# Expert regions cleared one batch sooner, experts chosen on logits, the last gate half first, one matrix addition a step

## What is computed

```python
x = x + ffn0(attention(x))       # layer 0
x = x + ffn1(lora_linear(x))     # layer 1

# attention: 8 query heads, 4 key/value heads of 64, a window of 256 in a paged cache
# ffn0: logits = clip(x @ gate_w.T, -50, 50); the top 2 of 8, softmax over those 2
#       expert e's matrix = W + 4096 weighted cells, scattered at mask_idx
# ffn1: probs = softmax(x @ gate_w); the top 2 of 8, scores divided by their sum, times alpha
#       expert e: fc2(gelu(fc1(x)))
```

## Time and profile before

| | us |
|---|---|
| median of 3 timed runs | 1142.62 (1139.97 to 1144.23) |
| the profiled execution, its own time | 1142.49 |
| its span, first to last instruction | 1140.7 |
| PE busy | 999.9 (88%) |
| DVE busy | 535.7 (47%) |
| ACT busy | 405.5 (36%) |
| POOL busy | 306.6 (27%) |

### The profile page before, as it was taken

How to read it: one execution, slowest core, us unless ns; L and a number is a source line. 1 busy time by engine, 2 the same in 40 slices (tenths; PEclk the granted TensorE clock), 3 DMA queues, 4 the chain that set the end, 5 groups by cost and what they waited for, 6 DMA issues and landing times.

```text
span 1140.7 us, 18892 instructions
## 1 busy us (share of the span) xinstructions
PE 999.9 (88%) x5042; PEld 678.0 (59%) x5043; DVE 535.7 (47%) x2106; ACT 405.5 (36%) x1185; POOL 306.6 (27%) x250
## 2 busy tenths in 40 slices
PE   5999949899999899808889997999289999999994
PEld 2464447677777677604444445666167777777772
DVE  5768874455455677442334442555423333333331
ACT  3434313555565555301111111112124444444440
POOL 3000140357654141111334440233202221122221
PEclk9989956899999999958999998999689999999998
DMA  8756540354453343238787745884443333333330
GB/s 266 238 215 214 198 162 21 94 131 112 127 157 114 112 153 112 75 130 228 210 221 125 137 84 166 303 332 160 149 139 67 68 62 72 72 65 67 57 59 2
DMA packets 82417, 156.25 MB, mean 137 GB/s; under 512 B 16023, under 2 KB 28999, under 8 KB 80768
## 3 DMA queue, kind: packets, MB, share of 16 engines
q1 hardware_dynamic: 40336, 86.99, 23.2%
q0 software_dynamic: 25520, 45.11, 19.1%
q10 hardware_dynamic: 16512, 23.60, 6.5%
HBM read 94.05 MB, written 73.19 MB: 147 GB/s over the span
## 4 chain that ended last, share of the span: by engine, by line
PE 64%; DVE 14%; issue 8%; DMA 7%; DVEq 2%; ACT 2%; SPq 2%; POOL 0%; ACTq 0%; POOLq 0%
PE ps L630 44%; PE ps L711 7%; PE ps L636 4%; DMA acc<-R,tok_i 4%; PE ps L701 3%; PE ps L694 3%; DVE R L1334 1%; DVE R L1326 1%; DVE R L1344 1%; PE ps L875 1%; DMA R<-rows 1%; DVE R L1337 1%; ACT R L977 1%; SPq L392 1%; SPq L391 1%
## 5 line engine op out<-in xcount | busy, mean ns | idle before, releaser
L630 PE MATMUL ps<-R 128*128 128x128 f32 (+4 forms) x2640 | 676.4, 413 | 20.1 <-DMA R<-in_x_t 11.5
L630 PEld LDWEIGHTS ps<-R 128*128 128x128 f32 x2640 | 395.9, 194 | 259.3 <-issue 242.4
L636 PE MATMUL ps<-ident,R 128*128 128x128 f32 x504 | 77.8, 286 | 67.2 <-DMA R<-rows 54.4
L602 POOL DMA_INDIRECT out_x<-R,tok_i x39 | 60.9, 1562 | 252.2 <-DVEq L1773 165.1
L530 POOL DMA_INDIRECT rows<-R,slot_i x64 | 67.1, 1048 | 203.5 <-DVEq L1521 180.6
L636 PEld LDWEIGHTS ps<-ident,R 128*128 128x128 f32 x504 | 62.2, 152 | 94.9 <-issue 77.1
L711 PEld LDWEIGHTS ps<-R 128*128 128x128 f32 x768 | 96.4, 199 | 20.0 <-ACT R L993 16.6
L711 PE MATMUL ps<-R 128*128 128x64 f32 x768 | 99.4, 281 | 4.8 <-ACT R L993 4.8
L1410 DVE CUSTOM_DVE_ANT_0 R<-ps,R 128x384 f32<-128x384 f32 x128 | 66.0, 553 | 75.2 <-issue 75.0
L987 ACT ACTIVATE R<-R,nmx 128x384 f32<-128x384 f32 x128 | 77.5, 607 | 58.8 <-DVE nmx L1410 58.7
L602 POOL DMA_INDIRECT acc<-R,tok_i x39 | 60.6, 1553 | 128.4 <-DVE R L1675 123.3
(11 more groups left out here) (281 smaller groups left out, 924.8 us busy)
## 6 DMA issues: line engine op xcount, KB each, us to landing
R<-rows SPq DMA_DIRECT2D x78, 258.0 KB, 3.4
R<-in_fc ACTq DMA_DIRECT2D x16, 1024.0 KB, 5.6
m_buf<-R SPq DMA_DIRECT2D x8, 1024.0 KB, 5.1
R<-m_buf SPq DMA_DIRECT2D x16, 512.0 KB, 3.9
R<-acc SPq DMA_DIRECT2D x32, 256.0 KB, 5.4
rows<-zrow SPq DMA_DIRECT2D x16, 258.0 KB, 3.7
new_kv<-R SPq DMA_DIRECT2D x16, 256.0 KB, 2.1
qn<-R SPq DMA_DIRECT2D x16, 256.0 KB, 2.5
```

The source lines that it names most:

```text
L602: po.indirect_dma_start(out=sums[s], out_offset=bass.IndirectOffsetOnAxis(ap=tok_i[:, s:s + 1], axis=0), in_=y_sb[s], in_offset=None, boun ...
L630: m = pe.matmul(out, lhs(k), rhs(k), start=(k == 0 and first), stop=(k == KC - 1 and last))
L636: m = pe.transpose(out[:, k * P:(k + 1) * P], src[:, k * P:(k + 1) * P], ident[:])
```

## The change

Six edits. (1) `ends`, split off from `tiles`, writes `end_i` and counts up `r_end` after the placing of the seventh batch. The zeros that SP writes there are 384 rows to an expert in place of 128 (up to 256 rows of the last batch may come before the 128), SP no longer waits for them, and POOL waits for them before it sends the last batch. (2) `choose` compares and multiplies in one operation per tile, which makes ten steps of it. Layer 1 chooses on the logits; the only exponential left is of the difference of the top two, `soft(i - 1)`, inside ACT's next pair. (3) At the end of attention PE projects the last tile's high half first, into bank 2, and the low half into bank 3. ACT in place of DVE copies the two halves out. (4) POOL issues 9 `cells` a round in rounds 1 and 2 and 10 in round 3. (5) DVE makes one addition in each step from period 4 step 2 on and the last two after `tiles`; SP fetches two pieces ahead of its `bk` wait and two behind it, from b = 4 on, and the first two at b = 3. (6) The loop over periods 1 to 4 is written out.

```diff
-            with eng.Fori(0, 2) as i:
-                period(2 * i + 1, "mid", 1, i)
-                period(2 * i + 2, "mid", 0, i)
...
+            for B in range(NB):
+                period(B, "first" if B == 0 else "last" if B == NB - 1 else "mid", B % 2, (B - 1) // 2)
...
             for b in range(NB - 1):
+                for m in range(4 * b - 14, 4 * b - 12) if b >= 4 else ():
+                    sp.wait_ge(S["m_done"], m - 1)
+                    fetch_m(m)
                 sp.wait_ge(S["bk"], uses(b, "mid" if b else "first")["q0"] + 1)
...
-                if b == 4:
+                if b == 3:
                     sp.wait_ge(S["mscat"], 16 * ST)
                     for m in range(2):
                         fetch_m(m)
-                if b >= 5:
-                    for m in range(7 * (b - 5) + 2, min(7 * (b - 4) + 2, 16)):
-                        sp.wait_ge(S["m_done"], m - 1)
-                        fetch_m(m)
+                for m in range(4 * b - 12, 4 * b - 10) if b >= 4 else ():
+                    sp.wait_ge(S["m_done"], m - 1)
+                    fetch_m(m)
...
                 for e in range(NE):
-                    end = sp.value_load(end_i[0:1, e:e + 1], min_val=0, max_val=ROWS - P * NE)
-                    sp.dma_start(rows_d[bass.ds(end, P), :].rearrange("p (h n) -> p h n", h=2),
-                                 zrow[:].unsqueeze(1).broadcast_to([P, 2, DX // 2])).then_inc(S["zrows"], 16)
-                sp.wait_ge(S["zrows"], 16 * NE * n)
+                    end = sp.value_load(end_i[0:1, e:e + 1], min_val=0, max_val=NE * REGION - 3 * P)
+                    sp.dma_start(rows_d[bass.ds(end, 3 * P), :].rearrange("(p a) (h n) -> p (a h) n", a=3, h=2),
+                                 zrow[:].unsqueeze(1).broadcast_to([P, 6, DX // 2])).then_inc(S["zrows"], 16)
...
-                t = 4 + 7 * (b - 1)
-                add = b <= 4
+                t = 4 + 9 * (b - 1)
+                add = b <= 3
...
-                    cells(t + 6)
+                    for u in range(t + 6, t + 9 if b < 3 else ST):
+                        cells(u)
             for b in (NB - 2, NB - 1):
                 po.wait_ge(S["r_slot"], b + 1)
+                if b == NB - 1:
+                    po.wait_ge(S["zrows"], 16 * NE)
                 for t in (2 * b, 2 * b + 1):
+                    if t == NT - 1:
+                        po.wait_ge(S["e_row"], 2)
...
-            project(at, "a1")
-            project(at, "h1")
+            pe.wait_ge(bc, at["o1"] + 1)
+            half("h1", 2).then_inc(S["e_in"], 1)
+            half("a1", 3).then_inc(S["e_in"], 1)
...
+                    if s == 0 and (not isinstance(i, int) or i > 0):
+                        soft(i - 1)
...
-                    TT(t1[:], src[:], b3(best2[:, c, :]), ALU.is_equal)
-                    ve.drain()
-                    TT(t1[:], t1[:], rb(rev[:]), ALU.mult)
+                    if c == 1:
+                        gap = TT(diff[:], best2[:, 1, :], best2[:, 0, :], ALU.subtract)
+                        if layer == 1:
+                            gap.then_inc(S["r_l"], 1)
+                    for t in range(2):
+                        ve.scalar_tensor_tensor(t1[:, t, :], src[:, t, :], best2[:, c, t:t + 1], rev[:], ALU.is_equal, ALU.mult)
...
+            def ends():
+                ve.drain()
+                CP(end_i[:], run[:])
+                ve.drain().then_inc(S["r_end"], 1)
...
-            ADDS = (2, 1, 2, 1, 1, 1, 1, 1)
...
                     if j == 7 and last:
+                        ends()
                         row_low(at, "a2", 2 * B)
-                    if isinstance(B, int) and 8 * B + j >= 42:
-                        for _ in range(ADDS[j]):
-                            next(adds, None)
+                    if 8 * B + j >= 34:
+                        next(adds)
...
                         for _ in place1(i - 1):
                             pass
+                        if not more:
+                            ends()
```

More of the change, by code:

```diff
@@ L281, in program @@
                 "last": ("a0", "h0", "o1", "a1", "h1", "o0", "rt", "a2"),
-                "after": ("h2", "o1", "a1", "h1", "rt")}
+                "after": ("h2", "o1", "rt")}
         NF, NM, NL = (len(USES[k]) for k in ("first", "mid", "last"))
@@ L290, in periods @@
         def periods(eng, period):
-            period(0, "first", 0, 0)
-            with eng.Fori(0, 2) as i:
-                period(2 * i + 1, "mid", 1, i)
-                period(2 * i + 2, "mid", 0, i)
-            period(5, "mid", 1, 2)
-            period(6, "mid", 0, 2)
-            period(NB - 1, "last", 1, 0)
+            for B in range(NB):
+                period(B, "first" if B == 0 else "last" if B == NB - 1 else "mid", B % 2, (B - 1) // 2)
         block = ctx.enter_context(nc.Block())
@@ L381, in _ @@
                         fetch_m(m)
-                if b >= 5:
-                    for m in range(7 * (b - 5) + 2, min(7 * (b - 4) + 2, 16)):
-                        sp.wait_ge(S["m_done"], m - 1)
-                        fetch_m(m)
+                for m in range(4 * b - 12, 4 * b - 10) if b >= 4 else ():
+                    sp.wait_ge(S["m_done"], m - 1)
+                    fetch_m(m)
+            for m in range(14, 16):
+                sp.wait_ge(S["m_done"], m - 1)
+                fetch_m(m)
             def zero_ends(n):
@@ L615, in _ @@
                 po.wait_ge(S["r_slot"], NB + b + 1)
+                if b == NB - 1:
+                    po.wait_ge(S["zrows"], 16 * NE * 2)
                 for t in (2 * b, 2 * b + 1):
@@ L719, in tail, with half @@
                 turn4(ps[:, 0, :], o_sb).then_inc(bk, 1)
+            def half(x, b):
+                lo, hi = (0, D // 2) if x[0] == "a" else (D // 2, DG)
+                return chunks(ps[:, b, 0:hi - lo], lambda k: o_t[:, k, :], lambda k: w_o[:, k, lo:hi])
             def project(at, x):
                 wait(pe, bc, at[x])
-                if x[0] == "a":
-                    chunks(ps[:, 0, 0:D // 2], lambda k: o_t[:, k, :], lambda k: w_o[:, k, 0:D // 2]).then_inc(bk, 1)
-                else:
-                    chunks(ps[:, 0, 0:DG - D // 2], lambda k: o_t[:, k, :], lambda k: w_o[:, k, D // 2:DG]).then_inc(bk, 1)
+                half(x, 0).then_inc(bk, 1)
             def cell_sums(at):
@@ L1039, in _ @@
             o_out(uses(NB, "after"), "1")
+            ac.wait_ge(S["e_lg"], 1)
+            ac.activation(a_rows[:, NT - 1, D // 2:D], ps[:, 2, 0:D // 2], ACT.Copy).then_inc(S["e_row"], 1)
+            ac.wait_ge(S["e_in"], 2)
+            ac.activation(a_rows[:, NT - 1, 0:D // 2], ps[:, 3, 0:D // 2], ACT.Copy).then_inc(S["e_row"], 1)
             ac.wait_ge(S["xs_sc"], 32 * NT)
@@ L1083, in soft @@
                 ac.wait_ge(S["r_l"], i + 1)
-                ac.activation(lg[:].rearrange(flat), lg[:].rearrange(flat), ACT.Exp).then_inc(S["r_lexp"], 1)
+                ac.activation(ew[:, 0, :], diff[:], ACT.Exp).then_inc(S["r_lexp"], 1)
             def outs(i, more=True):
@@ L1096, in _ @@
                 load_fc(fc2, fc2_v, 2 * i, S["fc2_d"])
-                soft(i)
                 load_fc(fc2, fc2_v, 2 * i + 1, S["fc2_d"])
@@ L1492, in place @@
                 ve.drain()
-                if layer == 0:
-                    TT(diff[:], best2[:, 1, :], best2[:, 0, :], ALU.subtract)
-                else:
-                    TT(diff[:], best2[:, 0, :], best2[:, 1, :], ALU.add)
-                    ve.drain()
-                    ve.reciprocal(rs2[:], diff[:])
-                    ve.drain()
-                    TT(best2[:], best2[:], rs2[:].unsqueeze(1).broadcast_to([P, 2, 2]), ALU.mult)
                 TT(t1[:], pre.rearrange("p (t e) -> p t e", e=NE), rb(run[:]), ALU.add)
@@ L1507, in place @@
                 TT(run[:], run[:], t2[:, 0, :], ALU.add)
+                if layer == 1:
+                    TS(rs2[:], ew[:, 0, :], 1.0, None, ALU.add)
                 ve.drain()
                 TT(run[:], run[:], t2[:, 1, :], ALU.add)
+                if layer == 1:
+                    ve.reciprocal(best2[:, 0, :], rs2[:])
                 yield
+                ve.drain()
                 TT(t3, chosen_e[:], t1[:].unsqueeze(1).broadcast_to([P, 2, 2, NE]), ALU.mult)
+                if layer == 1:
+                    TT(best2[:, 1, :], best2[:, 0, :], ew[:, 0, :], ALU.mult)
                 ve.drain()
```

21 lines of the change are left out of this document (6 added, 15 removed).

## The result

The changed kernel takes **1161.01 us** (median of 4 runs, 1156.85 to 1165.1) against 1143.42 for the kernel before on the same chip (4 runs). The ratio is 1.0154, 95% interval 1.0135 to 1.0173: slower by 1.5%, and outside the range that was given. The profiled run took 1159.31 us, 16.8 more than the profiled run of the kernel before.

What follows compares the result with a forecast made beforehand. PE's work was taken to bound most of the kernel, so edits gain only where PE stands still. From 1142.49 us: -10.3 + 9.8 + 10.5 - 6.7 - 0.3 = +3.0, so 1145.5 us, range 1134 to 1152.

Steps and rivals of the forecast that it cites:

- X: Both expert layers: time from issue of the first zeros to landing of the last, 24.8 us (23.6 to 26.1).
- Rival (d): Both layers: zeros come at 290 GB/s or less under a longer queue, 3.2 us lost in each, 1151.9 us; chance 13%.
- What stands behind X: After the zeros land: the last batch's four sends, their landing and SP's step to the rows' fetch, 8.1 us.
- Layer 0, -10.3 us: Way from attention to the first expert layer: earlier zeros bring the rows' fetch to 504.4 in place of 514.72.
- layer 1, +9.8: Way from the linear layer to the second expert layer: rows fetched at 838.3 in place of 828.52, +9.8 us.
- The cells and fetches in attention: Periods 3 to 4: the chain of cell DMAs and SP's fetch put the first addition at 347.5, +10.5 us.
- The cover: Attention: period 4's 10.5 us wait for the first addition absorbs PE's stall in period 3, so nothing is counted for it.
- Attention's sum: Attention: +10.5 us for the late first addition in period 4, -6.7 for the removed stall of period 5.
- Rival (b): Attention, period 4: the first piece is there in time and nothing stalls, 1135.0 us; chance 10%.
- Rival (c): Attention: the clock falls after the waits of periods 3 and 4, neither absorbed, +2.7 to 5.4 us; chance 15%.
- Rival (a): Both layers: zeros faster at 351 GB/s, landing in 20.6 us, both ways gain 4.2, 1137.1 us; chance 15%.
- the Trainium skill's formula: Zeros in both layers: a DMA takes 2.0 us plus bytes at 436 GB/s, giving 19.0 us and 1133.9; chance 5%.

Runs made afterwards that it cites:

- the fourth kernel: The changed kernel with zeros, matrix cells, SP's fetches and additions as before, leaving the choice, layer 1's softmax, half gate and written-out loop: 1144.29 us, ratio 0.9922.
- section 1: Four kernels undoing or isolating edits on one chip; the 35.2 us is from the changed kernel with layer 1's zeros as before, 1152.71 us, ratio 1.001.

## Why the prediction was wrong

- **The time X of the zeros is the step that failed.** "X is between 23.6 and 26.1 us; I take the middle, 24.8": it was 30.9 in layer 0 and 32.2 in layer 1 (to 0.3 us ahead of POOL's send). The bytes were right (7.40 MB, 7.41 in the trace) and the rate was wrong: 239 GB/s over the stretch, not 314. At 47 to 48 ns a piece, as in the kernel before, 16 engines write some 345 GB/s, which fits the 351 that was read; in the long stream the slow pieces raise the mean to 70 ns. The 314 and 351 were read from windows of 2 and 0.5 us of a transfer that was never long: eight blocks of 258 KB, 1.3 us apart. A rate that was seen with a third of the bytes was taken for all. Since both layers carry X, the miss counts twice: 6.1 + 7.4 = 13.5 us of the 13.8 between forecast and result (1145.5 and 1159.31, by the profiled runs). That the rest is so small is luck: single misses of about 1 us each way cancel (attention 1.4 better than forecast by the seventh placing, the stretch from the first fetch to layer 1's seventh placing 1.0 slower).
- **Rival (d) was the right one**, with the place and the sign, and the 290 GB/s that it was priced with still too high. Its mechanism, a longer queue, is at most a part: one block in flight brings the mean piece from 77 to 58 ns, not to 48, and pieces on 256 B boundaries stay at 40 with the queue as long. It had 13% and should have had more, because the only rows that spoke for a high rate were short ones.
- **What stands behind X was right.** 8.1 us; measured 0.3 + 7.86 in layer 0, 0.3 + 7.85 in layer 1. First zeros after the placing: 1.06 us forecast, 1.53 and 1.36 measured; the 0.3 that the shorter choice was to save there did not show.
- **Layer 0, -10.3 us, came out as -3.7** from the seventh placing (472.84, 2.4 late) to the fetch, **layer 1, +9.8, as +17.5.** That the two cancel was a property of the X that was chosen: they do so only near 24.8.
- **"Worth nothing while the zeros last beyond it"** was right for the half gate and the choice: the last batch is placed at 491.11 and POOL waits until 505.60. That these edits would count if the zeros ended sooner was right as well: the fourth kernel, which has little else, gains 0.8%. Which of its edits (the choice, the softmax, the half gate, the loop written out) brings it was not tried.
- **The cells and fetches in attention were right, and to the number by luck.** Cell 31 at 340.5, measured 340.48; the second `over_rows` at 318.3, measured 318.38; first addition at 347.5, measured 348.36. In between, single terms miss by up to 3.3 us and cancel: cell 11 came at 254.30 in place of 255.71, and the waits beside SP's two bursts fell on cells 19 and 26 (6.63 and 7.52 us), not 18 and 27. PE's stall in period 3 was put at 2 to 6 us and is 6.60, and the clock fell behind it. The Trainium skill's rule ("DMA: Bandwidth & Descriptors", "Queues, rings and completion order"), by which a cell would hardly wait behind SP's burst, was weighed and rightly set aside: those 6.63 and 7.52 us stand against 3.35. The cover held: the start of the queries is 9.2 us late, not 9.2 + 6.6. Period 4 took 43.7 us (45 forecast) and the next ones 34.9 (34.6).
- **Attention's sum**, +3.8 by 430.99, was +2.8 there and +0.6 at its end (480.90 against 480.32). The last 2.2 us were not in the sum. 1.7 of them are a slow clock: the kernel before took 3.68 us for the projection that began at 469.30 (granted clock 0.67 in its window of 4 us), the changed one has 1.99 us for it at 471.56 (1.00). Rival (b) fell, since the first piece came late. Rival (c) came half true: the clock fell in period 3 only.
- **Rival (a) and the Trainium skill's formula** ("DMA: Bandwidth & Descriptors", the anatomy of one DMA; X of 20.6 and 19.0) were furthest off. The page fits the formula to single DMAs issued by POOL, and the zeros are eight at a time, issued by SP. Its 436 GB/s is not reached by these pieces in any run; the best mean here, with aligned pieces, is 313.

With X at 31.5, near the mean of the two, the same sum would have given 1145.5 + 13.4 = 1158.9 us.

## What to carry to other kernels

A rate read in a short window of a small transfer is no rate for a long one: look whether the row covers as many bytes as the edit will move, and if none does, put the range around that and not around the spread of the rows that are there. Making a transfer start earlier by making it three times as large pays only while its end stays ahead of what waits for it; work out that end first. Where a long stream is written in pieces of about 1 KB, try rows padded to a multiple of 256 B, or pieces that are longer: here both were quicker, 27.0 and 24.5 us in place of 31. A mean price of a piece can hide a fast majority and a slow tail, so look at single pieces before you take it for a fixed cost.

## What the runs showed of the hardware

- A long stream of writes to memory in 1032 B pieces off 256 B boundaries has 257 to 344 GB/s for some 10 us and then 202 to 285 (changed kernel, first layer); 768 B pieces on such boundaries keep 318 to 338 GB/s to the end of theirs. The slower stream is a matter of some pieces: median 49 and mean 70 ns, against 39 and 40. Whether it is the start, the end or the boundary shared by two neighbours, whether 256 B or a smaller boundary counts, and why the decline takes so long, was not tried and stays open. The pitch of the rows and the size of the pieces changed with it.
- The same zeros took 30.9 us on the result's chip and 35.2 on that of section 1.
- The share of busy DMA engines does not show how fast a stream is. It is 1.10 at 235 GB/s and 1.03 at 318 GB/s: only the GB/s beside it does.
- Two queues that issue at once bring the time of issue from 10.98 to 6.11 us, and a block's landing goes from 3.5 to between 6.0 and 7.2 us.
